# Three normalisations of a batch moved from VectorE to ScalarE, and an earlier load of the softmax sums, in a transformer-and-Mamba layer

## The reference

```python
    x = L0_attn_x
    xn = _layernorm(x, axis=-1)
    x = x + _L0_attn_ref(xn, ...) + _L0_ffn_ref(xn, ...)

def _L0_ffn_ref(x, w_ln1, w_ln2, ...):
    def rmsnorm(x, w):
        norm = jnp.sqrt(jnp.mean(x * x, axis=-1, keepdims=True)) + EPS
        return x / norm * w
    x = x + mla(rmsnorm(x, w_ln1), ...)   # causal attention, 16 heads of 16, rotary halves
    x = x + moe(rmsnorm(x, w_ln2), ...)   # one shared expert and the best 2 of 7
    return x
```

## Time and profile before

| | us |
|---|---|
| median of 3 runs (4742.58 to 4753.63) | 4745.45 |
| the profiled execution | 4747.28 |
| its span, first to last instruction | 4745.5 |

### The profile page before, as it was taken

One profiled execution on the slowest core, in us unless ns is written; L12 is line 12 of the kernel. 1 busy time (PEld: TensorE's weight loads), 2 busy tenths in 40 slices (PEclk: granted clock), 3 DMA queues, 4 the chain that ended last, 5 costly groups with the idle time before them and its releaser, 6 DMA issues.

```text
span 4745.5 us, 71982 instructions
## 1 busy us (share of the span) xinstructions
PE 3827.0 (81%) x22840; PEld 2875.3 (61%) x22840; DVE 3217.3 (68%) x5803; ACT 2386.6 (50%) x6217; POOL 2250.6 (47%) x1204
## 2 busy tenths in 40 slices
PE   5887888888788775999688788888888888878886
PEld 2444444444444443777567777777777777777776
DVE  3555555555555532222189999999999999999997
ACT  0333333333333331333367767677676776776764
POOL 3233222322332311000167777777776777777674
PEclk7898889898888887999889899998999999989998
DMA  3222222222222213666412222222222222222221
GB/s 92 84 73 77 88 79 73 73 87 87 83 83 73 73 44 112 210 210 208 148 61 75 77 73 84 73 82 70 77 79 77 78 82 74 78 75 73 83 70 43
DMA packets 268633, 420.13 MB, mean 89 GB/s; under 512 B 60245, under 2 KB 232662, under 8 KB 245656
## 3 DMA queue, kind: packets, MB, share of 16 engines
q1 hardware_dynamic: 255896, 380.98, 24.8%
q0 software_dynamic: 12288, 33.57, 2.0%
HBM read 330.56 MB, written 83.10 MB: 87 GB/s over the span
## 4 chain that ended last, share of the span: by engine, by line
DVE 19%; POOL 12%; PE 10%; issue 9%; DVEq 1%; ACT 1%; DMA 0%; SPq 0%; POOLq 0%; ACTq 0%
POOL m_ub L1526 9%; PE m_Y L1891 4%; DVE m_S L1744 4%; DVE m_S L1752 4%; DVE m_PR L1744 4%; PE m_Y L1901 3%; DVE m_PR L1752 3%; DVE m_sp_v L1721 2%; POOL m_yg L1536 1%; PE m_Y L1904 1%; DVE m_ub L1729 1%; POOL m_dtx L1505 1%; DVE m_yz L1763 1%; PE m_F L1845 0%; DVE m_st L1700 0%
## 5 line engine op out<-in xcount | busy, mean ns | idle before, releaser
L1526 POOL TENSOR_TENSOR m_ub<-m_Bb,m_dtx 128x2048 f32<-128x2048 f32 x256 | 1156.7, 4541 | 550.6 <-PE m_Y L1891 544.2
L1641 ACT ACTIVATE m_dA<-m_dt,m_a_neg 128x128 f32<-128x128 f32 x4096 | 1213.3, 399 | 29.4 <-DVE m_S L1752 25.5
L1891 PE MATMUL m_Y<-m_ub,m_ident 128*128 128x128 f32 x8192 | 1013.8, 288 | 241.1 <-DVE m_ub L1729 238.8
L1891 PEld LDWEIGHTS m_Y<-m_ub,m_ident 128*128 128x128 f32 x8192 | 994.5, 204 | 250.3 <-DVE m_ub L1729 246.6
L529 ACT ACTIVATE f_pt<-f_X 128x512 f32<-128x512 f32 (+1 forms) x704 | 373.7, 556 | 844.4 <-PE f_X L816 792.3
L584 DVE TENSOR_REDUCE f_nm<-f_Y 128x1 f32<-128x512 f32 (+3 forms) x896 | 435.5, 532 | 343.2 <-PE f_Y L810 278.2
L809 PE MATMUL f_Y<-f_kst,f_qst 96*128 96x512 bf16 (+3 forms) x1024 | 289.3, 336 | 236.1 <-DVE f_nm L584 219.1
L1744 DVE SCALAR_TENSOR_TENSOR m_PR<-m_dA,m_S 128x512 f32<-128x512 f32 x512 | 355.6, 695 | 119.6 <-POOL m_ub L1526 48.8
L479 POOL TENSOR_TENSOR f_kq<-f_ra,f_rb 128x512 f32<-128x512 f32 x64 | 81.1, 1268 | 655.8 <-DVE f_rb L619 486.6
L1744 DVE SCALAR_TENSOR_TENSOR m_S<-m_dA,m_PR 128x512 f32<-128x512 f32 x512 | 354.8, 693 | 12.0
L809 PEld LDWEIGHTS f_Y<-f_kst,f_qst 96*128 96x128 bf16 x1024 | 110.1, 108 | 409.6 <-DVE f_nm L584 286.6
(11 more groups left out here) (237 smaller groups left out, 6690.9 us busy)
## 6 DMA issues: line engine op xcount, KB each, us to landing
m_Bb<-m_bc_dram SPq DMA_DIRECT2D x64, 1024.0 KB, 4.7
m_Cb<-m_bc_dram SPq DMA_DIRECT2D x64, 1024.0 KB, 4.7
f_parts_dram<-f_parts SPq DMA_DIRECT2D x32, 768.0 KB, 4.2
f_kst<-f_parts_dram SPq DMA_DIRECT2D x192, 128.0 KB, 2.6
f_qst<-f_parts_dram SPq DMA_DIRECT2D x192, 128.0 KB, 2.6
e_rows<-sorted_rows SPq DMA_DIRECT2D x70, 256.0 KB, 2.7
e_wg<-Wg SPq DMA_DIRECT2D x70, 256.0 KB, 2.9
e_wu<-Wu SPq DMA_DIRECT2D x70, 256.0 KB, 4.0
```

The costliest lines, as they stand in the source:

```text
L1526: pool.tensor_tensor(ub[:, h, i, :, :], Bb[:, s, :, :], dtx[:, par, m, None, s * SN:(s + 1) * SN].to_broadcast([P, NST, SN]), ALU.mult).th ...
L1641: last = act.activation(dA[:, h, i, n, :], dtt[:, par, m, s * SN:(s + 1) * SN], ACT.Exp, scale=a_neg[:, m, n:n + 1])
L1891: last = pe.matmul(Y[:, i * SN:(i + 1) * SN], ident[:, :], ub[:, h, i, n, :], start=False, stop=(n == NST - 1), skip_group_check=True)
```

## The change

Three normalisations of a batch are computed by ScalarE, with one activation per tile: out = scale * in + shift, both per partition. For h1 and xn that needs the shift -mean * factor, so GpSimd's chain of a batch gets three more small multiplies (steps 7, 8 and 10 of 10; the factor itself is step 9), and a constant -1. h2 has a scale only. VectorE keeps the reciprocals and the two copies of mvx. Two items are new, h1a (13) and h2a (30), for ScalarE's share; xn stays at its place and is ScalarE's. The order of items is changed as well: sl1 from 4 to 0, so ahead of stack1; rp1 from 10 to 6, ro1 from 12 to 7, rl1 from 16 to 12; T from 14 to 15, lat from 17 to 18, ym1 from 22 to 18, scat 1 from 18 to 19, the kq items of the first half one later; wo from 26 to 25 and split 0 from 25 to 26; nmt and d 1 one later.

```diff
@@ -142,20 +142,21 @@
...
-    for n, kind, i, j in ((0, "xload", 0, 0), (0, "mvx", 0, 0), (1, "stack1", 1, 0), (4, "sl1", 1, 0), (8, "bn", 0, 0), (10, "rp1", 1, 0), (11, "h1", 0, 0),
-                          (12, "ro1", 1, 0), (12, "scat", 0, 0), (14, "T", 0, 0), (16, "rl1", 1, 0), (17, "lat", 0, 0), (18, "scat", 1, 0), (20, "kq", 0, 0), (22, "ym1", 1, 0),
-                          (23, "kq", 0, 1), (25, "split", 0, 0), (26, "wo", 0, 0), (28, "mid", 0, 0), (29, "h2", 0, 0), (31, "xrload", 0, 0),
...
+    for n, kind, i, j in ((0, "xload", 0, 0), (0, "mvx", 0, 0), (0, "sl1", 1, 0), (1, "stack1", 1, 0), (6, "rp1", 1, 0), (7, "ro1", 1, 0), (8, "bn", 0, 0),
+                          (11, "h1", 0, 0), (12, "scat", 0, 0), (12, "rl1", 1, 0), (13, "h1a", 0, 0), (15, "T", 0, 0),
+                          (18, "lat", 0, 0), (18, "ym1", 1, 0), (19, "scat", 1, 0), (21, "kq", 0, 0), (24, "kq", 0, 1), (25, "wo", 0, 0),
+                          (26, "split", 0, 0), (28, "mid", 0, 0), (29, "h2", 0, 0), (30, "h2a", 0, 0), (31, "xrload", 0, 0),
...
@@ -460,16 +462,19 @@
...
+                chain(sc_step, 10, b, 7, tt(sc1[:, 8, :], mv[:, :, 0], consts[:, 3, :], ALU.mult))
+                chain(sc_step, 10, b, 8, tt(sc1[:, 9, :], sc1[:, 8, :], sc1[:, 1, :], ALU.mult))
...
-                tt(sc1[:, 7, :], sc1[:, 1, :], sc1[:, 6, :], ALU.mult).then_inc(sc_step, 1)
+                chain(sc_step, 10, b, 9, tt(sc1[:, 7, :], sc1[:, 1, :], sc1[:, 6, :], ALU.mult))
+                tt(sc1[:, 10, :], sc1[:, 8, :], sc1[:, 7, :], ALU.mult).then_inc(sc_step, 1)
...
@@ -531,6 +536,26 @@
+            if kind == "h1a":
+                sc1 = sc1_[:, parity(kind, r), :, :]
+                act.wait_ge(x_loaded, 16 * (b + 1))
+                act.wait_ge(sc_step, 10 * b + 10)
+                for t in range(TT):
+                    last = act.activation(h1[:, t, :], xm[:, t, :], ACT.Identity, scale=sc1[:, 7, t:t + 1], bias=sc1[:, 10, t:t + 1])
+                last.then_inc(h1_done, 1)
+            if kind == "xn":
+                act.wait_ge(xn_done, 2 * b + 1)
+                act.wait_ge(xr_loaded, 16 * (b + 1))
+                act.wait_ge(xs_ready, b)
+                for t in range(TT):
+                    last = act.activation(xn[:, t, :], xr[:, t, :], ACT.Identity, scale=mvx[:, 0, t:t + 1], bias=mvx[:, 1, t:t + 1])
+                last.then_inc(xn_done, 1)
+            if kind == "h2a":
+                act.wait_ge(rms2_rec, b + 1)
+                act.wait_ge(scattered, 16 * TT * TOPK * b)
+                for t in range(TT):
+                    last = act.activation(h2[:, t, :], x2[:, t, :], ACT.Copy, scale=sc2[:, 4, t:t + 1])
+                last.then_inc(h2_done, 1)
...
@@ -602,15 +627,8 @@
             if kind == "h1":
-                dve.wait_ge(sc_step, 7 * b + 6)
+                dve.wait_ge(sc_step, 10 * b + 6)
                 dve.reciprocal(sc1[:, 6, :], sc1[:, 5, :]).then_inc(rms_rec, 1)
...
-                dve.wait_ge(sc_step, 7 * b + 7)
-                for t in range(TT):
-                    last = dve.tensor_scalar(h1[:, t, :], xm[:, t, :], mv[:, t, 0:1], sc1[:, 7, t:t + 1], ALU.subtract, ALU.mult)
-                last.then_inc(h1_done, 1)
...
             if kind == "h2":
                 dve.wait_ge(sc2_step, 4 * (b + 1))
                 dve.reciprocal(sc2[:, 4, :], sc2[:, 3, :]).then_inc(rms2_rec, 1)
-                dve.wait_ge(rms2_rec, b + 1)
-                dve.wait_ge(scattered, 16 * TT * TOPK * b)
-                for t in range(TT):
-                    last = dve.tensor_scalar(h2[:, t, :], x2[:, t, :], sc2[:, 4, t:t + 1], None, ALU.mult)
-                last.then_inc(h2_done, 1)
```

More of the change, by code:

```diff
@@ L67, in build_attn @@
     before = sb("f_before", [P, ER, ER])
-    consts = sb("f_consts", [P, 3, TT])
+    consts = sb("f_consts", [P, 4, TT])
     xm = sb("f_xm", [P, TT, DM])
@@ L73, in build_attn @@
     mv_ = sb("f_mv", [P, 2, TT, 2])
-    sc1_ = sb("f_sc1", [P, 2, 8, TT])
+    sc1_ = sb("f_sc1", [P, 2, 11, TT])
     mvx = sb("f_mvx", [P, 2, TT])
@@ L143, in build_attn @@
                     S2_ITEMS.append(("oc", g - 1, 0))
-    STAGE = {kind: 2 for kind in ("xload", "bn", "h1", "T", "lat", "kq", "split", "mid", "keep", "stack")}
+    STAGE = {kind: 2 for kind in ("xload", "bn", "h1", "h1a", "T", "lat", "kq", "split", "mid", "keep", "stack")}
     STAGE.update({kind: 1 for kind in ("stack1", "s1", "nm", "nmt", "v")})
     STAGE.update({kind: 0 for kind in ("mvx", "xrload", "xn", "s2", "pv", "oc", "so", "sl", "rp", "ro", "rl", "ym")})
-    STAGE.update({kind: -1 for kind in ("sl1", "rp1", "ro1", "rl1", "ym1", "wo", "h2", "ht", "route", "lg", "rank", "pfx", "g", "u", "d")})
+    STAGE.update({kind: -1 for kind in ("sl1", "rp1", "ro1", "rl1", "ym1", "wo", "h2", "h2a", "ht", "route", "lg", "rank", "pfx", "g", "u", "d")})
     STAGE["scat"] = -2
@@ L151, in build_attn @@
     AT = {}
-    for n, kind, i, j in ((0, "xload", 0, 0), (0, "mvx", 0, 0), (1, "stack1", 1, 0), (4, "sl1", 1, 0), (8, "bn", 0, 0), (10, "rp1", 1, 0), (11, "h1", 0, 0),
[4 rows of a table removed]
-                          (47, "kq", 1, 1), (47, "pfx", 0, 0), (49, "split", 1, 0), (50, "nm", 0, 0), (51, "d", 0, 0), (52, "nmt", 0, 0), (53, "mid", 1, 0),
-                          (54, "d", 1, 0), (58, "keep", 1, 0)):
+    for n, kind, i, j in ((0, "xload", 0, 0), (0, "mvx", 0, 0), (0, "sl1", 1, 0), (1, "stack1", 1, 0), (6, "rp1", 1, 0), (7, "ro1", 1, 0), (8, "bn", 0, 0),
+                          (11, "h1", 0, 0), (12, "scat", 0, 0), (12, "rl1", 1, 0), (13, "h1a", 0, 0), (15, "T", 0, 0),
+                          (18, "lat", 0, 0), (18, "ym1", 1, 0), (19, "scat", 1, 0), (21, "kq", 0, 0), (24, "kq", 0, 1), (25, "wo", 0, 0),
+                          (26, "split", 0, 0), (28, "mid", 0, 0), (29, "h2", 0, 0), (30, "h2a", 0, 0), (31, "xrload", 0, 0),
+                          (32, "keep", 0, 0), (33, "ht", 0, 0), (35, "route", 0, 0), (36, "lg", 0, 0), (36, "xn", 0, 0), (37, "g", 0, 0), (37, "stack", 0, 0),
+                          (39, "u", 0, 0), (40, "rank", 0, 0), (42, "g", 1, 0), (43, "u", 1, 0), (45, "kq", 1, 0),
+                          (47, "kq", 1, 1), (47, "pfx", 0, 0), (49, "split", 1, 0), (50, "nm", 0, 0), (51, "d", 0, 0), (53, "mid", 1, 0), (53, "nmt", 0, 0),
+                          (55, "d", 1, 0), (58, "keep", 1, 0)):
         AT.setdefault(n, []).append((kind, i, j))
@@ L447, in _ @@
         fixed(pool.memset(consts[:, 2, :], 1e-5))
+        fixed(pool.memset(consts[:, 3, :], -1.0))
         fixed(pool.memset(va[:, :, :, HD:HD + 1], 1.0))
@@ L462, in do @@
                 pool.wait_ge(stats_done, TT * (b + 1))
[L463 to L468, removed]
+                chain(sc_step, 10, b, 1, tt(sc1[:, 0, :], mv[:, :, 1], consts[:, 2, :], ALU.add))
+                chain(sc_step, 10, b, 2, tt(sc1[:, 1, :], sc1[:, 0, :], consts[:, 0, :], ALU.pow))
+                chain(sc_step, 10, b, 3, tt(sc1[:, 2, :], mv[:, :, 1], sc1[:, 1, :], ALU.mult))
+                chain(sc_step, 10, b, 4, tt(sc1[:, 3, :], sc1[:, 2, :], sc1[:, 1, :], ALU.mult))
+                chain(sc_step, 10, b, 5, tt(sc1[:, 4, :], sc1[:, 3, :], consts[:, 1, :], ALU.pow))
+                chain(sc_step, 10, b, 6, tt(sc1[:, 5, :], sc1[:, 4, :], consts[:, 2, :], ALU.add))
+                chain(sc_step, 10, b, 7, tt(sc1[:, 8, :], mv[:, :, 0], consts[:, 3, :], ALU.mult))
+                chain(sc_step, 10, b, 8, tt(sc1[:, 9, :], sc1[:, 8, :], sc1[:, 1, :], ALU.mult))
             if kind == "h1":
@@ L518, in _ @@
         pool.wait_ge(scattered, 16 * TT * TOPK * BATCH)
-    N_CONST = 27
+    N_CONST = 28
     @block.scalar
@@ L592, in do @@
                     dve.bn_stats(st6[:, t, :], xm[:, t, :]).then_inc(stat1, 1)
-                dve.wait_ge(sc_step, 7 * b)
+                dve.wait_ge(sc_step, 10 * b)
                 if not isinstance(b, int) or b >= 2:
@@ L604, in do @@
             if kind == "h1":
-                dve.wait_ge(sc_step, 7 * b + 6)
+                dve.wait_ge(sc_step, 10 * b + 6)
                 dve.reciprocal(sc1[:, 6, :], sc1[:, 5, :]).then_inc(rms_rec, 1)
-                if not isinstance(b, int) or b > 0:
-                    dve.wait_ge(*used(("T", 0), before_(r)))
-                    dve.wait_ge(*used(("T", 1), before_(r)))
-                dve.wait_ge(sc_step, 7 * b + 7)
-                for t in range(TT):
-                    last = dve.tensor_scalar(h1[:, t, :], xm[:, t, :], mv[:, t, 0:1], sc1[:, 7, t:t + 1], ALU.subtract, ALU.mult)
-                last.then_inc(h1_done, 1)
             if kind == "kq":
@@ L630, in do @@
             if kind == "mvx":
[L631 to L638, removed]
-                for t in range(TT):
-                    last = dve.tensor_scalar(xn[:, t, :], xr[:, t, :], mvx[:, 0, t:t + 1], mvx[:, 1, t:t + 1], ALU.subtract, ALU.mult)
-                last.then_inc(xn_done, 1)
+                dve.wait_ge(sc_step, 10 * b + 8)
+                dve.wait_ge(xn_done, 2 * b)
```

(2 more changed lines are left out.)

## The result

The changed kernel takes 4636.5 us (median of 4 runs, 4631.5 to 4647.4) against 4749.5 us before: a ratio of 0.977 (0.974 to 0.979), 113 us less. The prediction was 4705 us, and its range began at 4640. All executions behind the numbers of this document are fast ones; one of the four of r3 took 16489 us and is left out. The profiled execution took 4631.5 us, its span 4629.6.

A forecast was written before the change was run, and what follows sets the result against it. TensorE was taken as nearest to full, losing 13.7 us a round waiting for VectorE's row maxima. Terms 3.1 + 0.8 - 0.8 gave 3.1 us over 13 rounds, 40 us: 4705 us median, range 4640 to 4752.

The forecast's parts named there:

- part 5: Remaining moves, including ym1 between the two scatter halves, priced at nothing; first three rounds lose 4 us, last three win 4.
- absorbed: Rival, chance 0.20: ScalarE's wait near the scatters' end swallows the gain ahead of it; 0.4 us a round left, 4740 us.
- My last condition: Sign that the forecast is wrong: the end of GpSimd's scatters fixes when ScalarE resumes behind the transposes of h1.
- Part 1: Softmax sums loaded right behind x, landing about 858.2, bounds 857 and 860; with h1's move 3.1 us a round.
- Part 2: h1's scaling on ScalarE, 2.3 us for four activations; transposes of h1 start 3.0 us sooner in the round examined.
- Part 3: h2 on ScalarE, waiting behind residual sum, split and mid: gain 0.8 us a round, bounds 0 and 1.2.
- stall B goes whole: Rival, chance 0.07: TensorE's 5.30 us idle during h2's scaling vanishes if split does not gate h2; 4 us more a round, 4653.
- Part 4: xn on ScalarE puts 2.3 us ahead of VectorE's tanh: cost between 0 and 2.3 us a round, 0.8 taken.
- What would show it: Signs in the later profile: x loads 105 to 106 us apart, sums' wait at most 1.5 us, several predicted engine waits.
- the clock stays up: Rival, chance 0.15: spreading TensorE's idle time keeps its clock up, another 3 us a round, 4665 us.
- Sums late: Rival, chance 0.12: sums land late ahead of VectorE's maxima; at 864.0 a round loses 2.7 us, 4780 us.
- the ends: First and last rounds of the attention stage: 4 us lost at the start, 4 us won in the last three, evening out.

The follow-up runs named there:

- r3: Kernel before with h2 alone computed on ScalarE, nothing else moved, on chip B: 4638.6 us against 4746.5, ratio 0.977.
- e6: Kernel before with only the second four scatters moved behind the multiply of the shares, chip B: 4669.1 us against 4749.5, ratio 0.984.
- e3: Changed kernel with the second four scatters back directly behind the first four, multiply of the shares behind them, chip A: 4693.3 us, ratio 0.988 to the kernel before.
- e4: Kernel before with only the four steps of the sums (sl1, rp1, ro1, rl1) moved early, chip A: 4720.8 us against 4749.4, ratio 0.992.
- e7: Changed kernel with h1 alone back on VectorE, chip B: 4640.3 us, ratio 0.978 to the kernel before.
- e5: Changed kernel with split put ahead of wo again, chip B: 4548.6 us, ratio 0.959 to the kernel before.
- e8: Changed kernel with split ahead of wo, h1 and xn on VectorE, only h2 on ScalarE, chip B: 4562.1 us, ratio 0.962 to the kernel before.
- r2: Changed kernel repeated without any edit, chip B: 4614.2 us against 4746.5 for the kernel before, ratio 0.975.
- e10: Kernel before with scatters in rows of six and two instead of eight in a row, chip C: 4673.7 us against 4675.0, ratio 1.000.
- e9: Kernel before with h2 alone computed on ScalarE, nothing else moved, on chip C: 4564.7 us against 4675.0, ratio 0.977.

## Why the prediction was wrong, step by step

**The step that failed** is the first sentence of part 5: ym1 between the two halves of the scatter, "Nothing". It is worth 80 us by e6 on chip B, more than the 69 us by which the forecast missed, and 57 us by e3 from the other side. I had the row in hand: ScalarE's wait of 4.49 us that ends 1.7 us behind the last scatter. I read it as a fixed point that could swallow another part's gain (the rival "absorbed") and didn't ask what it costs itself, nor what a change that takes the row of scatters apart does to it. My last condition ("if the scatter's end fixes when ScalarE resumes") was the right one to name: with the row apart the point is gone, and in e4, with the row in place, part of the gain was lost. What the move of the second half does by itself I had put at nothing, without a reason.

**Part 1** held as to its mechanism: sums behind x, no wait in the round shown, 9.0 us in 800. In the four rounds where VectorE did wait, it resumed 7.5 to 8.2 us behind the load of x; the forecast landing, 858.2, is 7.8 behind it. By e4 the sums alone are 29 us. **Part 2** is off in size: load to T lost 0.8 us, not 2.5, and h1 on ScalarE adds nothing to the sums (e7). h1 itself took 2.07 us, less than the 2.3 from the row. The estimate from the formula in ScalarE: Activation LUTs, What ACT_TABLE_LOAD costs, in the Trainium skill, was 2.06 us; this trace agrees.

**Part 3** was right in its chain and near in size: 0.1 us longer with 1.4 us more work in it, so 1.3 us against 0.8 forecast, just past the bound of 1.2. It explains why the rival "stall B goes whole" stayed away, and e5 shows that this was the place to earn. Why h2 is slow on VectorE can be read in the kernel before. Its four instructions stand beside GpSimd's residual sum (906.23 to 908.57) and L493 (908.53 to 910.69), and single ones take from 0.34 to 2.2 us:

```profile
L675 DVE TENSOR_SCALAR f_h<-f_xn,f_sc x44: 340/1222/2204, 361.1 to 1454.2; 128x256 f32<-128x256 f32 x44
```

In that round the first ends at 908.72 and the second at 910.84, each 0.15 us behind the end of a GpSimd instruction, and the two that have no GpSimd instruction beside them take 0.34 us each. On ScalarE, beside the same residual sum in e5, the four take 1.7 us. SBUF — State Buffer, section SBUF: two separate sides, in the Trainium skill, says that a VectorE instruction in a 2-port mode and a GpSimd instruction take a shared pair of ports in turn, each for its whole length, and that ScalarE never waits for it. No row names the mode, but the times agree.

**Part 4**: xn on ScalarE puts 2.07 us ahead of the tanh, for which VectorE then waits 3.2 us instead of 0.85. What that costs isn't settled: e5 and e8, which differ in xn and h1, are 14 us apart in favour of ScalarE, and their intervals overlap.

**What would show it** came out nearly point by point and so didn't point at the missing term: the wait ahead of s1.2.0 is 1.37 us (near 1.5 forecast), T's wait for h1 1.04 (just over the 1), L491 stands right behind L512, and TensorE's waits for maxima, exponential and h2 add up to 1.90 + 1.52 + 0.86 = 4.3 us (near 4). VectorE's longest wait for the sums was 2.6 us, not 1.5. Only the distance of the loads of x, 102.7 us instead of 105 to 106, told of the term that was missing.

**The sum.** Without the scatters' part the change is worth 33 us (4669.1 of e6 less 4636.5 of the first comparison) or, by r2 on e6's own chip, 55 us, and 56 on chip D, where no such wait is seen in the changed kernel. The forecast was 40, so the terms that I had costed came near as a whole. Their places were off: a round is 2.0 us shorter than in e6 in the first trace (4.6 in r2's), not 3.1, and the ends, which I set even, gave another 13: from the last load of x to the last ht 302 us before, 286 in e6, 273 after. **The rival "the clock stays up"** named 4665 and came nearest by number. That is luck: over 500 to 1300 us the clock rose only from 0.90 to 0.92, and e6 gained 80 us by a move that the rival doesn't contain. How much of the gain came back through the clock no run separates. "Sums late" fell: they landed where the forecast had them.

## What to carry to other kernels

Price each move of an item on a queue, also one into slack: look at a round in which that item doesn't run and compare. A wait that nothing in the profile explains is a cost to be explained, before it is used as a limit for others. And moving work to an engine that does it faster helps only if that engine isn't held up ahead of it: put before it only what is ready, as the split was with its place ahead of wo.

## What the runs showed of the hardware

On chips A and B, VectorE and ScalarE started on scores up to 4.6 us (e3) after TensorE's record of them had ended (a modelled end), while GpSimd issued the later ones of eight indirect DMAs, 1.27 us apart. On chip C the same instructions ran at the same pace (1.27 us in e10), rows of eight (e9) and six (e10) left no such wait, and the kernel before was 1.6% faster. D had the kernel before at that faster time (1.5%), but no row of eight was traced there. One kernel shows the difference by itself: h2 alone, with eight scatters in a row, took 4638.6 us on B (r3) with 77 us of "remote" waits, and 4564.7 on C (e9) with none. Kernels without that row take nearly the same on both kinds: e5 4548.6 on B and 4546.2 on D, the changed kernel 4614.2 on B and 4623.1 on D. So a gain can belong to a chip: the change is worth 113 to 132 us on one kind and 56 us on the other. Only B was used twice, so that the difference lies in the chip, and not in something that changed between the sessions, is likely but not shown.
